# A decoder's last expert stage, rebuilt: row tiles sorted by blocks of four experts instead of all tokens through all experts

## The reference, cut to what matters

```
logits = x @ gate_w.T;  scores = sigmoid(logits);  choice = scores + gate_bias
# 32 experts in 4 groups of 8: keep the 2 groups with the largest sum of their top two
# of the 16 experts left, the 8 largest are chosen, weight = score / sum(scores) * 2.5
y = sum over the 8 chosen experts of weight * (silu(x @ wg.T) * (x @ wu.T)) @ wd.T   # 256 -> 128 -> 256
y += shared expert, the same form with an inner width of 256
out = h + y         # x above is the layer norm of h
```

## Time and profile before

| | us |
|---|---|
| median of 3 runs (2393.60 to 2399.07) | 2398.31 |
| the profiled execution, span from first to last instruction | 2400.5 |
| TensorE busy in it (27613 matmuls) | 2194.1 |
| VectorE (DVE) busy | 1549.6 |
| ScalarE (ACT) busy | 1181.3 |
| GpSimd (POOL) busy | 749.0 |
| first matmul of stage F | 1788.2 |
| last matmul of stage F starts | 2389.3 |

### The profile page before, as it was taken

How to read it: one execution, slowest core, us unless ns; L and a number is a source line. 1 busy time by engine, 2 the same in 40 slices (tenths; PEclk the granted TensorE clock), 3 DMA queues, 4 the chain that set the end, 5 groups by cost and what they waited for, 6 DMA issues and landing times. The chain is left out here.

```text
span 2400.5 us, 65663 instructions
## 1 busy us (share of the span) xinstructions
PE 2194.1 (91%) x27613; PEld 1812.9 (76%) x27613; DVE 1549.6 (65%) x3455; ACT 1181.3 (49%) x3280; POOL 749.0 (31%) x916
## 2 busy tenths in 40 slices
PE   5899999999989999739996999999977999999998
PEld 4688888888867888628994666666655888888887
DVE  5877667767544665466762766746657777777776
ACT  4645554455226776505652666757752333333332
POOL 3444324432324444325885434201010110101100
PEclk9999999999999999959997999999978999999999
DMA  4010101011002000023445000000000000000001
GB/s 140 32 38 12 38 29 38 12 38 42 30 30 90 20 20 19 21 78 91 122 80 124 2 2 2 2 2 2 2 9 14 27 21 26 27 21 27 21 8 36
DMA packets 87974, 83.57 MB, mean 35 GB/s; under 512 B 27264, under 2 KB 83456, under 8 KB 86272
## 3 DMA queue, kind: packets, MB, share of 16 engines
q1 hardware_dynamic: 81536, 70.98, 9.4%
q0 software_dynamic: 6144, 8.39, 2.1%
HBM read 68.71 MB, written 10.65 MB: 33 GB/s over the span
## 5 line engine op out<-in xcount | busy, mean ns | idle before, releaser
L2743 PE MATMUL bank<-f_XH,f_wp 128*128 128x512 f32 x1088 | 364.5, 396 | 5.9 <-DVE f_XL L2853 5.9
L2743 PEld LDWEIGHTS bank<-f_XH,f_wp 128*128 128x128 f32 x1088 | 208.4, 192 | 48.8 <-issue 5.3
L2743 PEld LDWEIGHTS bank<-f_wp,f_Hp 128*128 128x128 f32 x1632 | 214.3, 191 | 27.5 <-DVE X L2880 16.0
L2743 PE MATMUL bank<-f_wp,f_Hp 128*128 128x256 f32 x1632 | 218.5, 283 | 16.2 <-DVE X L2880 15.4
L2927 POOL TENSOR_TENSOR f_wp<-wa,f_wp 128x768 fp32r<-128x768 f32 x34 | 62.9, 1851 | 524.6 <-ACT f_wp L2893 524.6
L2743 PE MATMUL bank<-f_XL,f_wp 128*128 128x512 f32 x544 | 215.8, 397 | 0.0
L2878 DVE SCALAR_TENSOR_TENSOR X<-bank,f_w,X 128x256 f32<-128x256 f32 x512 | 211.5, 477 | 0.0
L805 DVE SCALAR_TENSOR_TENSOR a_acc<-a_praw,a_convw,a_acc 128x256 f32<-128x256 f32 x345 | 200.1, 587 | 9.4 <-ACT a_acc L950 1.2
L2916 ACT ACTIVATE f_Hp<-f_H 128x512 fp32r<-128x512 f32 x136 | 86.0, 632 | 223.6 <-DVE f_H L2865 223.6
L2914 ACT ACTIVATE f_G<-bank 128x512 f32<-128x512 f32 x136 | 81.4, 599 | 165.4 <-PE bank L2743 165.4
L888 DVE COPY_PREDICATED wa<-masks,bank 128x512 f32<-128x512 uint8 x128 | 93.5, 733 | 102.8 <-PE bank L706 102.7
(11 more groups left out here) (388 smaller groups left out, 5507.8 us busy)
## 6 DMA issues: line engine op xcount, KB each, us to landing
wa<-in_c_w SPq DMA_DIRECT2D x64, 256.0 KB, 2.9
wa<-in_f_gu SPq DMA_DIRECT2D x34, 256.0 KB, 2.7
wb<-grown SPq DMA_DIRECT2D x4, 1536.0 KB, 7.7
a_KQg<-grown SPq DMA_DIRECT2D x4, 1536.0 KB, 7.0
wa<-in_f_d SPq DMA_DIRECT2D x34, 128.0 KB, 2.8
a_E<-decays SPq DMA_DIRECT2D x16, 256.0 KB, 4.0
X<-in_x SPq DMA_DIRECT2D x4, 512.0 KB, 5.9
wa<-in_a_wqkv SPq DMA_DIRECT2D x1, 2048.0 KB, 9.0
```

The costliest lines, as they stand in the source:

```text
L2743: i = t.e.matmul(out_, lhsT[x], rhs[y], start=n == 0 and k == 0, stop=n == 2 and k == nk - 1, skip_group_check=True)
```

## The change

**Blocks of four.** The 32 experts form 8 blocks of 4. A token belongs to a block if it chose at least one of its four. Each block has a region of 2048 rows in DRAM (`blocks`), a row being the 256 normed numbers, the 32 weights, the token's number and padding: 320 numbers, 1280 bytes.

**Routing in stage E.** As soon as a pair of token tiles is normed and transposed, its routing is done: `logits` on PE and ACT, then on DVE `logits`, `group`, `choose` (42 instructions a pair with `rank`, 10 of them MAX8), then `rank`, matmuls with a triangular matrix that give each row its place in each block: members from the front, others from the back. Then POOL sends the token tile by 8 indirect DMAs, one to each block, 128 in all. In E the first seven pairs are routed and 77 sends issued, 3.5 per step g from g = 13 on; the last pair and 51 sends come in F. PE gets 4 + 2 small matmuls a pair.

**Tiles.** F computes the shared expert on all tokens as before (8 passes). After that it works on 36 row tiles, whatever the data: one of 256 rows at the front of each block (8), then 11 of 512 and 17 of 256, given to blocks at run time by a table that DVE computes from the counts (`schedule`, 33 instructions at pass 5) and SP reads into registers. A tile takes 4 passes, one for each expert of its block. Its rows are loaded from DRAM by SP, transposed (`turn`: PE, ACT for the high part, DVE for the low part), a few DVE instructions fetch its weights (`prep`), and the results are collected in Y (ACT the first expert, DVE the other three) and added to the output in DRAM by one indirect DMA with addition on POOL for each 128 rows (`scatter`), 94 in all. The output first gets X after the shared expert.

**Weights.** A pass of a row tile needs its own expert's weights: 146 fetches of 384 KB instead of 34, four load buffers and five split buffers. The low part of the down weights (128 x 256) is always DVE's; that of the up weights (128 x 512) is DVE's for the first 14 fetches and POOL's after. The host lays the weights out as one array with rows of 3 KB.

The diff, cut to its core (function bodies named in the text above are cut to what carries them):

```diff
+NB4, EB = 8, 4
+SMALL, BIG = 2 * P, 4 * P
+NBIG, NSMALL = 11, 17
+RW = 320
...
+        def send(g, s):
+            _, n, b = s
+            g.wait_ge(row_ready.sem, row_ready.at[n // 2,])
+            route_emptied(g, "rank", n // 2)
+            g.e.indirect_dma_start(blocks, bass.IndirectOffsetOnAxis(ro.idx[:, n, b:b + 1], 0), rows[:, n, :], None,
+                                   bounds_check=NB4 * B * T - 1).then_inc(sent[b], 16)
...
+                c, k = (g - 9) // 4, (g - 9) % 4
+                if 0 <= c < NT // 2 - 1:
+                    order += [[("logits", c)], [("group", c)], [("choose", c)], [("rank", c)]][k]
+                if g > 12:
+                    order += sends[7 * (g - 13) // 2:7 * (g - 12) // 2]
...
-            NEX, NR, NQ = NE1 + NSH, 5, NT // 4
+            NEX, NR, NWP, NH_, LAG, EARLY = NE1 + NSH, 4, 5, 3, 2, 14
...
+            entries = sorted([((i + 0.5) / NBIG, i) for i in range(NBIG)] + [((i + 1) / NSMALL, NBIG + i) for i in range(NSMALL)])
+            entry = [None] * NB4 + [i for _, i in entries]
+            NTILE = len(entry)
+            slots = [BIG if i is not None and i < NBIG else SMALL for i in entry]
+            NP, NW = NSP + EB * NTILE, NSH + EB * NTILE
...
+                for k in range(NW):
+                    if k and first_pass(k) - 2 == p:
+                        order += [("split", k)]
+                if NSP - EB <= p < NP - EB:
+                    t, j = tile_of(p + EB)
+                    if j < slots[t] // SMALL:
+                        order += [("turn", t, j)]
+                    elif j == 2:
+                        order += [("prep", t)]
+                if LAG <= p < NP + LAG:
+                    order += [("down", p - LAG, half) for half in range(halves(p - LAG))]
                 if p < NP:
+                    order += [("part", p)]
+                t, j = tile_of(p - LAG - 1)
+                if t >= 0 and j == EB - 1:
+                    order += [("scatter", t)] + [s for s in late_sends if s[2] == t + 5]
...
+                        v.wait_ge(high_done.sem, high_done.at[k,])
+                        if k < EARLY:
+                            v.e.tensor_tensor(wp[:, 1, 0:2 * D], w[:, 0:2 * D], whole(wp[:, 0, 0:2 * D]),
+                                              ALU.subtract).then_inc(low_dve.sem, 1)
+                        v.e.tensor_tensor(wp[:, 1, 2 * D:], w[:, 2 * D:], whole(wp[:, 0, 2 * D:]), ALU.subtract).then_inc(low_down.sem, 1)
...
+                    elif what == "split" and s[1] >= EARLY:
+                        k = s[1]
+                        wp, w = Wp[k % NWP], wr[k % NR]
+                        g.wait_ge(high_done.sem, high_done.at[k,])
+                        g.e.tensor_tensor(wp[:, 1, 0:2 * D], w[:, 0:2 * D], whole(wp[:, 0, 0:2 * D]),
+                                          ALU.subtract).then_inc(split_done.sem, 1)
+                    elif what == "scatter":
+                        t = s[1]
+                        n = slots[t] // P
+                        downs_emptied(g, NSP + EB * t + EB - 1)
+                        g.wait_ge(prepared.sem, prepared.at[t,])
+                        g.wait_ge(out_begun, 64)
+                        if t:
+                            g.wait_ge(scattered, 16 * tiles_before[t])
+                        for m in range(n):
+                            g.e.indirect_dma_start(out_rows, bass.IndirectOffsetOnAxis(ido[t % 4][:, m:m + 1], 0),
+                                                   Y[t % 2][:, m, :], None, bounds_check=B * T - 1,
+                                                   compute_op=ALU.add).then_inc(scattered, 16)
...
-            for n in range(NT):
-                e.dma_start(out.rearrange("b (t p) d -> p (b t) d", p=P)[:, n, :], X[:, n, :]).then_inc(out_written, 16)
-            e.wait_ge(out_written, 16 * NT)
```

More of the change, by code:

```diff
@@ new lines, in route_start_dve @@
+        def route_start_dve(v):
+            ids = small[:, 3 * P:3 * P + 2 * NT].rearrange("p (n c) -> p n c", c=2)
+            v.wait_ge(const_in, 48)
+            v.step(v.e.memset(ro.before[:, 0, :], 0.0))
+            v.step(v.e.tensor_scalar(ro.late, ids[:, :, 0], -1.0, float(B * T), ALU.mult, ALU.add)); v.settle()
+            v.step(v.e.tensor_tensor(ro.late, ro.late, ids[:, :, 1], ALU.subtract)); v.settle()
+            v.step(v.e.tensor_scalar(rows[:, :, D + NE1], ro.late, -1.0, float(B * T), ALU.mult, ALU.add)); v.settle()
@@ L307, in stage_a @@
+        sends = [("send", n, b) for n in range(9) for b in range(NB4)]
+        sends += [("send", n, b) for b in range(3) for n in range(9, 14)] + [("send", n, b) for b in range(3) for n in (14, 15)]
+        sends += [("send", n, b) for b in range(3, NB4) for n in range(9, NT)]
+        SENT_AHEAD = 7 * (2 * NT + 3 - 13) // 2
         def stage_a(sx):
@@ L2391, in stage_e @@
                     continue
-                if what == "exp":
+                if what in ("exp", "send"):
+                    continue
+                if what in ("group", "choose"):
+                    plan_route(s)
                     continue
@@ L2413, in stage_e @@
                     continue
+                if what in ("logits", "rank"):
+                    plan_route(s, banks[i])
+                    continue
                 at[s] = banks[i]
@@ L2437, in tensor @@
                     what, b = s[0], at.get(s)
-                    if what in ("exp", "bias", "stat", "norm"):
+                    if what in ("exp", "bias", "stat", "norm", "group", "choose", "send"):
+                        continue
+                    if what in ("logits", "rank"):
+                        route_pe(t, s)
                         continue
@@ L2667, in stage_f @@
[L2667 to L2675 removed]
+            ex = [t_(f"ex{i}", [P, BIG // P, RW]) for i in range(2)]
@@ new lines, in stage_f @@
+            onehot, table = t_("onehot", [P, NDYN, NB4]), t_("table", [P, NDYN, 2], I32)
+            rest, full, cum, used, taken = (t_(n, [P, NB4]) for n in ("rest", "full", "cum", "used", "taken"))
+            steps, blk = t_("steps", [P, 2, NB4]), t_("blk", [P, NB4])
+            over, passed = t_("over", [P, NB4, NB4]), t_("passed", [P, NSMALL, NB4])
+            counts_made, table_ready = sem("f_counts_made"), sem("f_table_ready")
+            wr_in = [sem(f"f_expert_in{i}") for i in range(NR)]
@@ new lines, in stage_f @@
+            last_pass = lambda k: 4 * k + 3 if k < NSH else k - NSH + NSP
+            size = lambda p: 4 * P if p < NSP else slots[tile_of(p)[0]]
+            halves = lambda p: size(p) // (2 * P)
+            early = sends[SENT_AHEAD:]
+            order = [("split", 0), ("stat", "F", last), ("high", 0)] + [s for s in early if s[1] < NT - 2 and s[2] < 3]
+            order += [("high", 1), ("norm", "F", last)]
+            late_sends = [s for s in early if not (s[1] < NT - 2 and s[2] < 3)]
+            for p in range(NP + LAG + 2):
+                if p == 1:
+                    order += [("ln", "F", last), ("high", 2)]
+                elif p == 2:
+                    order += [("logits", last), ("high", 3)]
+                elif p == 4:
+                    order += [("rank", last)] + [s for s in late_sends if s[2] < 5]
+                if p < NP:
+                    order += [("up", p)]
@@ L2688, in stage_f @@
-                if p >= LAG:
-                    order += [("down", p - LAG, 0), ("down", p - LAG, 1)]
-            at = {}
+                    order += [("choose", last)]
+                elif p == 5:
+                    order += [("table",)]
+                for k in range(NW):
[7 more added lines that the diff above has]
+                        order += [("prep", t)]
@@ L2849, in vector @@
                         ln_dve(v, s)
+                    elif what in ("logits", "group", "choose", "rank"):
+                        route_dve(v, s)
+                    elif what == "table":
+                        schedule(v)
                     elif what == "high":
@@ L2909, in scalar @@
                         if p >= NH_:
[L2910 to L2916 removed]
+                            c.wait_ge(parts_ready.sem, parts_ready.at[p - NH_,])
```

614 lines of the change are left out of this document (437 added, 177 removed).

## The result

The kernel after takes 2464.22 us (2462.09 to 2474.47) where the kernel before took 2395.95 beside it: a ratio of **1.0296, 95% interval 1.0273 to 1.032**. Forecast were 2354, with a range to 2412. In the profiled executions the span goes from 2400.5 to 2472.6 us, +72.1: 2.9 before stage E, **56.7 in stage E** (first score matmul to first matmul of F, 206.1 to 262.8) and **12.5 in stage F** (612.3 to 624.8), which was to shrink by some 72 (the forecast's terms for F, with 6 of its start counted to E).

The account below looks back on a forecast made before the run. TensorE's matmuls were taken to bound stage F. Terms -119 + 45 + 3 + 22 - 4 + 12 - 3 = -44 on 2398.3 gave 2354 us; own range 2322 to 2386, to 80% from 2290 to 2412.

Parts of the forecast that it names:

- signs of being wrong: 256-row tiles at 9.2, or at 12.5 or more, ACT's weight copy waiting for a DMA, or E grown over 45 us.
- TensorE's work, -119: Stage F: 128 passes removed, row tiles and transposes added, -119 us if TensorE stays the bound.
- Does it?: Whether TensorE stays the bound in F's row tiles: 256-row tiles at 10.8 us against TensorE's 9.0, +45 us (0 to +96).
- +3: 512-row tiles of F: TensorE stays the bound, 0.3 us each for hand-overs, +3 us.
- late sends: Sends for blocks 5 to 7 follow scatters on POOL, the last two sets ahead of needed subtractions: +12 us (0 to 25).
- Routing in E, +22: Stage E: routing takes 8.8 us of DVE a pair against 8.0 free: +22 us (+8 to +45).
- The rival on the clock: 256-row tiles of F starve TensorE to 80%, some run in part at 1.2 GHz: +22 us; no chance given.
- Start of F: Stalls between stages, in the eight shared passes and before the first rows: 34 against 37 us, -4.
- End, -3: After the last matmul: two scatters and their landing, some 8 us, where it had been 11.2: -3 us.
- Fetches late: Rival for F's row tiles: weight fetches arrive late, 13.8 us a tile gives 2429 us; chance 0.10.
- The slower rival: DVE and POOL in turn at the weights' low parts in 256-row tiles: 12.8 us a tile, 2409 us; chance 0.13.
- The rule of the Trainium skill: DVE instructions with two SBUF inputs contend with GpSimd SBUF reads; first issuer holds the port: 2404 us all caught, 2309 none.

Follow-up runs that it names:

- f2: Kernel after with DVE subtracting all low parts of the up weights and POOL none: 2370.3 us, ratio 0.987 to the kernel before.
- f1: Kernel after with one scatter in each pass of the next tile instead of all of a tile's in a row: 2440.5 us, ratio 1.017.
- g4: Kernel after with all row sends moved from stage E to the start of F, run on chip 3: 2570.2 us.
- e2: Kernel after with all row sends moved from stage E to the start of F, run on chip 9: 2556.4 us.
- k1: Kernel after with no row sends in stage E and without the tie rule of the choice: 2511.7 us.
- h2: Kernel after with row sends moved to F and as many indirect transfers with 64-byte rows in their places in E: 2553.5 us.

## Why the prediction was wrong

It was off by 110 us. The profiled execution, the longest of the four, is 116 us over the forecast span (2472.6 against 2400.5 - 44): 50 lie in tiles 8 to 35 (428.3 against 378.3), 19.5 in tiles 0 to 7, 29 in E (56.7 against the 22 for routing and 6 for the wait at its end), 3 before E, 9 at the end, and 6 at the edges of these stretches. Of its own signs of being wrong one came: E grew by more than 45 us. DVE was busy 84% of tiles 8 to 35, where 90% or more in the 256-row ones was a sign of being right.

- **TensorE's work, -119: right.** With POOL out of the way (f2) tiles 8 to 35 hold 351 us of TensorE, where 17 x 9.0 + 11 x 17.4 = 344 were counted (the other stretches were not compared).
- **"Does it?", 10.8 us a 256-row tile: the step that failed.** It added up each engine's work of a tile and took POOL as free to do its 8.9 us in any order. One thing was left out and one priced too low. Left out, POOL's queue: the scatters stood ahead of a subtraction that is needed two passes later, 4 x 1.86 = 7.4 us behind each 512-row tile and 3.7 behind a 256-row one. Their time was in the sums, the wait was not; the "+3" for the 512-row tiles did not hold it at all. The same reasoning was used for the late sends and not here (27 us, f1).

  Priced too low, the port: 0.3 us were put on each of the eight subtractions of a 256-row tile, 17 x 2.4 = 41 us in tiles 8 to 35, and nothing on those of the 512-row tiles. Measured there were 77 us in the kernel after, 104 with the scatters spread (f1) and none without POOL's subtractions (f2). The two causes feed each other in one way: a backlog on POOL makes two subtractions run in a row, and DVE is held through both (4.09 us), ten times in these tiles. Without the backlog (f1) the long ones are gone, but more short ones come. The range's upper end, 12.8 a tile, had one whole POOL subtraction in each pass, but no queue.
- **Routing in E, +22 (8 to 45): too small, and the mechanism half told.** VectorE was full in bursts around `choose`, and delayed TensorE there as counted. What was not counted is that TensorE, the bound of this stage, would then run part of it at its lower clock (0.85 on average in g4, 0.93 before): +48 us without sends. The rival on the clock looked for this in F: there the clock was 0.94 in tiles 8 to 35, and TensorE's busy time 375.0 us against 351.5 at 1.00 in f2.
- **Sends in E:** they were weighed as POOL's time; that they can slow TensorE was not foreseen. On chip 9 E took 254.5 and 262.9 us with them (f1, f2) and 254.5 without (e2), on chip 3 312.3 and 254.6.
- **Start of F, right**: the shared passes were put at 33.4 + 15 + 8 = 56 us, and took 55.3.
- **Late sends, +12 (0 to 25)**: with POOL else free (f2) tiles 3 to 5 took 13.0, 13.4 and 12.8 us where their neighbours took 9.7, some 10 us. With subtractions behind the sends, tiles 2 to 4 took 15.1, 22.1 and 21.5, where the tiles after took 12: some 23. Near the upper end.
- **End, -3: wrong.** Two scatters and their landing were counted, some 8 us after the last matmul. It was 17, where it had been 11: four scatters of the tile before stand ahead of the last two (from 2452.06 and from 2462.43), which wait for them. POOL's queue again.
- **Fetches late: did not come.** In f2 the DMA engines moved 179 GB/s in tiles 8 to 35, 245 in tiles 0 to 7, with TensorE busy 97% and 91%.
- **The slower rival named the right pair of engines** and the right side, but as a loss in each pass; nearly half of the price (35 of 77 us) was paid in ten bursts after scatters, and the queue it did not have. The rule of the Trainium skill that was weighed (page "SBUF — State Buffer", section "Who interferes with whom") is borne out in that the two exclude each other: 418 ns alone against 785, all held subtractions end just after one of POOL's, and the instruction that reads PSUM is unharmed at 472 against 476. Who goes first the records do not settle: for 17 of the 60 held ones, DVE's recorded start lies before POOL's. With every pass caught it gave 2404, the nearest of the rule's two sums to the result.

## What to carry to other kernels

Before moving work to an engine, write its queue down in order for one period and ask of each item what stands ahead of it and how much lead it has; a sum per period hides a wait of four scatters behind which a needed subtraction stands. Where two engines share a port, the way out can be to give all of the work to the busier of them: DVE took 90 us more work and was busy for 35 us less (1624.9 against 1659.9, f2 and the kernel after). And in a stage that TensorE bounds with small matmuls, idle time of VectorE is not free room: the last 15 us of its work came with 37 (g4 against k1).

## What was not expected of the hardware

- A VectorE subtraction was held through two GpSimd subtractions in a row: 4.09 us instead of 0.68.
- Stage E with its sends took 253 to 263 us on three chips (9, 10, 14) and 302 to 322 on two (3, 12); without sends it took 254.6 on one of these two, and the kernel before took 2391.7 to 2403.6 us on all. Chip and occasion were not told apart. A gain measured on one chip (0.987) was a loss on another (1.019).
- An indirect DMA of 128 rows of 1280 bytes to DRAM holds POOL 0.97 us, and 0.30 to the next; 64-byte rows hold it as long (h2: POOL busy 95.97 us in E, with 1280-byte rows 96.00).
